# The next group's product with B moved ahead of the two products that finish a gate and up block, on VectorE

## The chip, the cores and the metric

One Trainium2 chip, one of its cores. The time is that of one launch on the device, in microseconds (us); lower is better. The engines are TensorE (PE; PEld is its weight load), VectorE (DVE), ScalarE (ACT), GpSimd (POOL) and SyncE (SP, which issues the DMAs here).

## What is computed

A block with two halves on 2048 tokens of 1024 channels, all in 32 bits. The first half is a selective scan (a state space layer), the second a gated feed-forward with low-rank (LoRA) additions:

```
h  = layernorm(x) * (1 + ca) + sa
xp = h @ x_proj_w.T                       # dt_in (32), B (16), C (16)
dt = softplus(dt_in @ dt_proj_w.T + dt_proj_b)
dA = exp(dt[..., None] * A);  dBx = dt[..., None] * B * h[..., None]
state = dA_t * state + dBx_t;  y_t = sum_n state[:, n] * C_t[n]      # over all tokens
x  = x + ga * (y + D * h)
h2 = layernorm(x) * (1 + cb) + sb
hidden = silu(gate(h2)) * up(h2)          # 1024 -> 2752, each with a LoRA term
x  = x + gb * down(hidden)                # 2752 -> 1024, with a LoRA term
```

The six modulation vectors come from `silu(c) @ wmod`, and `ga` and `gb` are kept away from zero.

## The kernel before

Channels lie on the 128 partitions (8 tiles), tokens in the free dimension. The tokens are cut into six chunks, `CH = [256, 320, 368, 368, 368, 368]`. While TensorE does the feed-forward of chunk c, the other engines do the scans of chunk c+1 and prepare chunk c+2.

**Units.** The feed-forward of a chunk is 71 units (`UNITS`): one `lora_a`, then in three parts the gate and up blocks of 128 hidden channels in turn (21 pairs and a last unit `both` with half a block each), `lora_down`, and eight `down` blocks. A unit is 24 or 25 matmuls for a gate or up block, since each 32-bit product is made of three with halved operands (high and low parts). TensorE writes a unit into one of four PSUM banks (`FP`); a fixed plan (`BANK`, `BEFORE`) says which, and which earlier use must be over (`bank_free`). The plan is made by program order.

**Groups.** The scans of a chunk are 64 groups: one of 16 states, one pair of channel tiles. For group n, VectorE makes the product with B (`dbx`, L1165: `ring <- hb * B`, B broadcast in PSUM by TensorE, L758), ScalarE makes two decays (L931), VectorE runs two scans (L1277), ScalarE keeps the last state (L948), GpSimd multiplies with C (L1414) and adds to y (L1373). The products lie in a ring of four places (`ring`); a place is free once GpSimd has added the group four before. VectorE makes the product of group n+1 just ahead of the scans of group n, both in the piece `("grp", c, n)`.

**Pieces.** Groups and the small steps of the coming chunk are spread over the units by weight (`PIECES[c][u]`). Every engine goes through the units in the same order and does, at unit u, its part of the pieces of u. The other steps that matter here: centering (`cen`, L1220) and its squares on ScalarE (L989), which TensorE sums (L735); the norm's factor (`rstd`, seed on ScalarE L996) and the product with it (`norm`, L1237); `dt` (L822), its exponent steps `sp` on ScalarE (to L1055), six products `soft` on VectorE (L1248 to L1257) and the copy `keep` (L1060); the C row copied by ScalarE (L941); low halves of weights and hidden blocks by GpSimd (L1421, L1430).

**A finished gate and up block.** For a pair of units gate j, up j: ScalarE makes the tanh of gate j (L1105) during unit up j, behind that unit's pieces. VectorE uses both in the unit after up j, by two calls of `used`: the gate's product (L1297: `(tanh + 1) * gate`), which waits for the tanh, and the up's (L1300: `0.5 * that * up`), which waits for TensorE's last matmul of the block (L877). With these two, here called the hidden products, the two banks are free. Then ScalarE rounds the result (L1117) and GpSimd makes its low half (L1430). For `both` the same is L1109, L1304 and L1307.

Of the kernel before, what the change touches and what calls it, by code (L numbers as in the profile page):

```python
# [77 lines left out]
NU = len(UNITS)  # L78
# [43 lines left out]
def group_id(c, n):  # L122
    return GROUPS * c + n
# [214 lines left out]
PIECES = [pieces_at(c) for c in range(CHUNKS)]  # L338
# [36 lines left out]
def build(nc, x_t, mod_w, cT, ident, x_proj, dt_proj, dt_bias, a_log, d_vec, w_la, w_gu, w_td, w_dn, out_t):  # L375
    w_dram = nc.dram_tensor("w_scratch", (NU, P, 2, SLOT), F32, kind="Internal").ap()

    with ExitStack() as ctx:
# [773 lines left out]
        def _(dve):  # L1152
# [38 lines left out]
                    away_from_zero(mod[:, GB, :]).then_inc(v_mod, 1)  # L1191
                dve.wait_ge(v_mod, n + 1)

            def piece(p):
                kind = p[0]
                if kind == "mod":
                    mod_vectors(p[1])
# [10 lines left out]
                elif kind == "late":  # L1208
                    blocks = LATES[p[1]]
                    n, at = blocks[0] // MOD_EACH, blocks[0] % MOD_EACH * MOD_COLS // P  # L1210
                    w = len(blocks) * MOD_COLS // P
                    dve.wait_ge(pe_col, blocks[-1] + 1)
                    V.tensor_copy(mod[:, n, at:at + w], FP[:, BANK["col", blocks[0]], 0:w]).then_inc(v_late, 1)
                elif kind == "cen":
                    _, k, c, q = p
                    if q == 0:
                        dve.wait_ge(pe_sum, ln_index(k, c) + 1)
                        if k == 0 and c >= 2:
                            dve.wait_ge(g_h2, PAIRS * (c - 1))
                    V.scalar_tensor_tensor(out=pair_of(hb, c, q), in0=over_pair(bank_of("sum", k, c)), scalar=-1.0 / D,  # L1220
                                           in1=ypair(c, q), op0=ALU.mult, op1=ALU.add).then_inc(v_cen, 1)
                elif kind == "rstd":
                    _, k, c = p
                    li = ln_index(k, c)
                    bank, row = bank_of("sq", k, c), seed[:, 0:CH[c]]
                    dve.wait_ge(a_rs, li + 1)
                    V.tensor_scalar(bank, bank, 1.0 / D, EPS, ALU.mult, ALU.add).then_inc(v_step, 1)
                    dve.wait_ge(v_step, 4 * li + 1)
                    V.scalar_tensor_tensor(out=bank, in0=bank, scalar=-0.5, in1=row, op0=ALU.mult, op1=ALU.mult).then_inc(v_step, 1)
                    dve.wait_ge(v_step, 4 * li + 2)  # L1230
                    V.tensor_tensor(bank, bank, row, ALU.mult).then_inc(v_step, 1)
                    dve.wait_ge(v_step, 4 * li + 3)
                    V.scalar_tensor_tensor(out=bank, in0=bank, scalar=1.5, in1=row, op0=ALU.add, op1=ALU.mult).then_inc(v_step, 1)
                    dve.wait_ge(v_step, 4 * li + 4)
                elif kind == "norm":
                    _, k, c, q = p
                    V.tensor_tensor(pair_of(hb, c, q), pair_of(hb, c, q), over_pair(bank_of("sq", k, c)), ALU.mult).then_inc(v_norm, 1)  # L1237
                elif kind == "xs":
                    c = p[1]
                    T = CH[c]  # L1240
                    dve.wait_ge(a_xs, c + 1)
                    V.tensor_tensor(xs[64:128, c % 2, 0:T], FP[64:128, BANK["proj", c], 0:T], xs[64:128, c % 2, 0:T].bitcast(F32), ALU.subtract).then_inc(v_xs, 1)
                elif kind == "soft":
                    _, c, i = p
                    T, t = CH[c], ND * c + i
                    bank = bank_of("dt", c, i)
                    dve.wait_ge(a_fac, NF * t + 1)
                    V.scalar_tensor_tensor(out=bank, in0=bank, scalar=FACTORS[0][1], in1=eb[:, t % 2, 0:T], op0=ALU.add, op1=ALU.mult).then_inc(v_soft, 1)  # L1248
                    for f in range(1, NF):
                        dve.wait_ge(a_fac, NF * t + f + 1)  # L1250
                        dve.wait_ge(v_soft, NF * t + f)
                        V.scalar_tensor_tensor(out=bank, in0=sqb[:, f - 1, 0:T], scalar=FACTORS[f][1], in1=bank, op0=ALU.add, op1=ALU.mult).then_inc(v_soft, 1)  # L1252
                    dve.wait_ge(v_soft, NF * (t + 1))
                    V.tensor_tensor(bank, bank, tile_of(dtb, c, i), ALU.add).then_inc(v_add, 1)
                    dve.wait_ge(v_add, t + 1)
                    dve.wait_ge(a_ini, PAIRS * c + i // 2 + 1)
                    V.scalar_tensor_tensor(out=tile_of(hb, c, i), in0=bank, scalar=modc(GA, i), in1=tile_of(hb, c, i),  # L1257
                                           op0=ALU.mult, op1=ALU.mult).then_inc(v_u, 1)
                elif kind == "first":
                    dbx(0, 0)  # L1260
                elif kind == "grp":
                    _, c, n = p
                    T = CH[c]
                    s, q = state_of(c, n)
                    g = group_id(c, n)
                    if group_after(c, n):
                        dbx(*group_after(c, n))
                    dve.wait_ge(v_dbx, g + 1)
                    if c and q == 0:
                        dve.wait_ge(a_save, 3 * NS + s + 1 if c == 1 else group_id(c - 1, n) + PAIRS)  # L1270
                    for a in range(2):
                        i = 2 * q + a
                        buf = ring_of(c, n)[:, a, :]
                        dve.wait_ge(a_da[a], g + 1)
                        if c == 0 and a == 0:
                            dve.wait_ge(a_da[1], g + 1)
                        V.tensor_tensor_scan(buf, decays(c, n, a), buf, hst[:, s * ND + i:s * ND + i + 1] if c else 0.0,  # L1277
                                             ALU.mult, ALU.add).then_inc(v_scan[a], 1)
                elif kind == "evac":
                    q, T = p[1], CH[0]  # L1280
                    dve.wait_ge(pe_y, NS * (q + 1))
                    dve.wait_ge(g_ini, PAIRS)
                    V.tensor_tensor(ypair(0, q), FP[:, 0, 0:2 * T].rearrange("p (a t) -> p a t", a=2), ypair(0, q), ALU.add).then_inc(v_ev, 1)
# [64 lines left out]
            for c in range(CHUNKS):  # L1348
                for u in range(NU):
                    g = c * NU + u  # L1350
                    last = UNITS[(g - 1) % NU][0]
                    if last == "up":
                        used(*divmod(g - 2, NU))
                    if g and last != "gate":
                        used(*divmod(g - 1, NU))
                    if UNITS[u][:2] == ("down", len(PARTS) - 1) and UNITS[u][2] == 0:
                        lora_low(c)
                    for p in PIECES[c][u]:
                        piece(p)
            used(CHUNKS - 1, NU - 1)  # L1360

        @block.gpsimd
# [146 lines left out]
```

## Time and profile before

| | |
|---|---|
| median of 3 runs | 2260.53 us (2260.38 to 2260.57) |
| the profiled execution's own time | 2265.11 us |
| its span | 2263.3 us |
| TensorE busy | 2026.9 us, 90% |
| GpSimd busy | 1558.3 us, 69% |
| VectorE busy | 1441.1 us, 64% |
| ScalarE busy | 1044.8 us, 46% |

The profiled execution is 4.6 us longer than the median. The units begin at 344 us; before that the modulation and the first chunk's scans are done. The chunks' units begin at about 344, 669, 998, 1337, 1676 and 1977 us. The last chunk's units run without any groups.

How a row is read: a time in microseconds from the span's start, a duration, engine, line, operation, output <- inputs, shapes; in brackets how long the engine had been idle before the instruction and what ended that.

### The profile page before, as it was taken

Reading aid. Unit: us, or ns where it says so; the run is one execution under the profiler, and the core shown is the slowest. Engines: PE = TensorE matmul, PEld = TensorE weight load, DVE = VectorE, ACT = ScalarE, POOL = GpSimd, SP = SyncE. Lnnn points to the kernel's source line nnn. Section 1 sums busy time; section 2 is a strip of 40 time slices with the busy share of each in tenths; the row PEclk is TensorE's granted clock in tenths of the full one; section 3 lists DMA queues with packets and bytes.
Section 4 is the critical chain, followed back from the end, with each engine's and each line's share of the span. In section 5 each row is a group of like instructions: output and inputs, shape, how many; then the busy total and the mean of one; then the engine's idle time right before and its main releaser. Section 6 shows DMA issues by size and latency. Waiting matters only on the chain.

```text
span 2263.3 us, 32653 instructions
## 1 busy us (share of the span) xinstructions
PE 2026.9 (90%) x11470; PEld 1836.5 (81%) x11470; DVE 1441.1 (64%) x2118; ACT 1044.8 (46%) x2337; POOL 1558.3 (69%) x968
## 2 busy tenths in 40 slices
PE   6597748888778889899999999999999999999999
PEld 3243227777768889899899889899889999999999
DVE  5676776778666778766778766778767774211111
ACT  3777765666453555444554443554444332210000
POOL 4679879999977877977877876877869886110100
PEclk8798768989999999999999999999999999999999
DMA  9799966778767677576667576667577877787786
GB/s 351 273 363 392 340 242 247 264 283 298 273 244 260 212 269 266 207 284 222 217 233 267 186 282 228 217 234 267 186 266 252 284 247 270 244 297 266 258 292 215
DMA packets 120051, 594.13 MB, mean 263 GB/s; under 512 B 10448, under 2 KB 22992, under 8 KB 80208
## 3 DMA queue, kind: packets, MB, share of 16 engines
q1 hardware_dynamic: 119888, 592.04, 73.4%
q8 instruction: 92, 1.51, 0.3%
q14 instruction: 71, 0.58, 0.1%
HBM read 506.97 MB, written 85.03 MB: 262 GB/s over the span
## 4 chain that ended last, share of the span: by engine, by line
PE 58%; DVE 17%; ACT 8%; POOL 7%; issue 7%; DMA 2%; DVEq 0%; ACTq 0%; SPq 0%; POOLq 0%
PE FP L852 48%; DVE ring L1277 7%; DVE ring L1165 3%; PE FP L735 3%; POOL ring L1414 3%; DVE FP L1252 2%; ACT SC L931 2%; POOL y L1373 2%; PE FP L877 1%; PE FP L813 1%; PE FP L769 1%; POOL xlo L1405 1%; DMA wts<-w_scratch 1%; DMA modw<-mod_w 1%; DVE hb L1237 1%
## 5 line engine op out<-in xcount | busy, mean ns | idle before, releaser
L852 PE MATMUL FP<-xhi,wts 128*128 128x368 f32 (+2 forms) x4224 | 1055.1, 326 | 72.2 <-ACT dtb L1060 20.9
L852 PEld LDWEIGHTS FP<-xhi,wts 128*128 128x128 f32 x4224 | 757.3, 194 | 81.1 <-issue 69.9
L1414 POOL TENSOR_TENSOR ring<-ring,c_row 128x736 f32<-128x736 f32 (+2 forms) x336 | 575.0, 1712 | 252.5 <-ACT hst L948 252.4
L852 PE MATMUL FP<-xlo,wts 128*128 128x368 f32 (+2 forms) x2112 | 685.0, 324 | 0.0
L931 ACT ACTIVATE SC<-dtb,aneg 128x368 f32<-128x368 f32 (+2 forms) x768 | 409.7, 539 | 574.5 <-DVE ring L1277 573.9
L852 PE MATMUL FP<-hhi,wts 128*128 128x368 f32 (+5 forms) x2376 | 572.6, 322 | 14.2 <-POOL hlo L1430 4.4
L1277 DVE TENSOR_TENSOR_SCAN ring<-SC,hst,ring 128x368 f32<-128x368 f32 (+1 forms) x640 | 579.9, 948 | 4.2 <-ACT SC L931 3.8
L1373 POOL TENSOR_TENSOR y<-y,ring 128x736 f32<-128x736 f32 (+1 forms) x320 | 555.6, 1736 | 13.9
L852 PEld LDWEIGHTS FP<-hhi,wts 128*128 128x128 f32 (+1 forms) x2376 | 408.5, 186 | 22.6 <-issue 10.0
L852 PEld LDWEIGHTS FP<-xlo,wts 128*128 128x128 f32 x2112 | 409.6, 194 | 1.1
L852 PE MATMUL FP<-hlo,wts 128*128 128x368 f32 (+5 forms) x1188 | 379.5, 319 | 0.0
L1165 DVE TENSOR_TENSOR ring<-hb,SC 128x736 f32<-128x736 f32 (+2 forms) x384 | 327.7, 853 | 62.9 <-PE FP L769 38.3
L1430 POOL TENSOR_TENSOR hlo<-hid,hhi 128x368 fp32r<-128x368 f32 (+4 forms) x132 | 122.4, 927 | 278.5 <-ACT hhi L1117 266.1
L852 PEld LDWEIGHTS FP<-hlo,wts 128*128 128x128 f32 (+1 forms) x1188 | 220.8, 186 | 2.3 <-issue 0.2
L1297 DVE SCALAR_TENSOR_TENSOR hid<-hid,FP 128x368 f32<-128x368 f32 (+2 forms) x126 | 64.2, 509 | 234.6 <-ACT hid L1105 230.4
L1323 DVE SCALAR_TENSOR_TENSOR y<-FP,mod,y 128x368 f32<-128x368 f32 (+2 forms) x144 | 80.9, 566 | 177.7 <-PE FP L852 177.3
L1300 DVE SCALAR_TENSOR_TENSOR hid<-hid,FP 128x368 f32<-128x368 f32 (+2 forms) x126 | 64.3, 510 | 152.7 <-PE FP L877 145.6
L948 ACT ACTIVATE hst<-ring 128x2 f32<-128x2 f32 x384 | 78.1, 203 | 141.0 <-DVE ring L1277 140.3
L758 PE MATMUL SC<-xs,sel 128*128 128x256 f32 (+2 forms) x144 | 66.1, 459 | 62.5 <-ACT c_row L941 25.6
L1105 ACT ACTIVATE hid<-FP 128x368 f32<-128x368 f32 (+2 forms) x126 | 55.4, 440 | 134.7 <-PE FP L877 134.5
L1117 ACT ACTIVATE hhi<-hid 128x368 fp32r<-128x368 f32 (+2 forms) x126 | 60.3, 479 | 119.1 <-DVE hid L1300 118.7
L758 PEld LDWEIGHTS SC<-xs,sel 128*128 128x128 f32 x144 | 30.2, 210 | 92.4 <-DVE ring L1165 31.5
(119 smaller groups left out, 2008.0 us busy)
## 6 DMA issues: line engine op xcount, KB each, us to landing
wts<-w_scratch SPq DMA_DIRECT2D x243, 1152.0 KB, 5.2
wts<-w_scratch SPq DMA_DIRECT2D x91, 896.0 KB, 4.9
wts<-w_scratch SPq DMA_DIRECT2D x51, 1024.0 KB, 5.8
w_scratch<-wts SPq DMA_DIRECT2D x43, 1152.0 KB, 8.2
modw<-mod_w SPq DMA_DIRECT2D x24, 1024.0 KB, 10.5
raw<-w_gu SPq DMA_DIRECT2D x29, 576.0 KB, 8.4
w_scratch<-wts SPq DMA_DIRECT2D x16, 896.0 KB, 8.6
w_scratch<-wts SPq DMA_DIRECT2D x9, 1024.0 KB, 6.0
```

What stands on the lines that cost most here:

```text
L735: last = mm(bank, ones[:, :], of[:, i, 0:T], start=(i == 0), stop=(i == ND - 1))
L758: mm(SC[:, BC0 + k % 2, 0:CH[c]], sel[:, at:at + 1].to_broadcast([P, P]), xs[:, c % 2, 0:CH[c]], start=True, stop=True).then_inc(pe_b, 1)
L852: last = mm(out, w, x, start=(start and k == 0 and e == 0), stop=(stop and k == n - 1 and e == 2))
L931: A(decays(c, n, a), tile_of(dtb, c, i), ACT.Exp, scale=aneg[:, i * NS + s:i * NS + s + 1]).then_inc(a_da[a], 1)
L948: A(hst[:, s * ND + 2 * q:s * ND + 2 * q + 2], ring_of(c, n)[:, :, T - 1], ACT.Copy).then_inc(a_save, 1)
L1165: V.tensor_tensor(ring_of(c, n), pair_of(hb, c, q), over_pair(SC[:, BC0 + k % 2, 0:T]), ALU.mult).then_inc(v_dbx, 1)
L1277: V.tensor_tensor_scan(buf, decays(c, n, a), buf, hst[:, s * ND + i:s * ND + i + 1] if c else 0.0, ALU.mult, ALU.add).then_inc(v_scan[a], 1)
L1300: V.scalar_tensor_tensor(out=h, in0=h, scalar=0.5, in1=bank, op0=ALU.mult, op1=ALU.mult).then_inc(v_used, 1)
L1323: V.scalar_tensor_tensor(out=y[:, c % 3, j, 0:T], in0=bank, scalar=modc(GB, j), in1=y[:, c % 3, j, 0:T], op0=ALU.mult, op1=ALU.add).then_i ...
L1373: G.tensor_tensor(ypair(c, q), ypair(c, q), ring_of(c, n), ALU.add).then_inc(g_add, 1)
L1414: G.tensor_tensor(buf, buf, over_pair(c_of(k)), ALU.mult).then_inc(g_hc, 1)
L1430: G.tensor_tensor(hlo[rows, k, 0:T], hid[rows, j % 2, 0:T], hhi[rows, k, 0:T].bitcast(F32), ALU.subtract).then_inc(g_hlo, 1)
```

## The change

At a unit that follows an up block, VectorE called `used` for the gate and for the up block first and then did the unit's pieces. Now, where such a unit has a group among its pieces, VectorE does the pieces that stand before the first group, then the product with B of the group after it, then the two calls of `used`, then the scans of the group. Units without a group, and units after another kind, keep their order. The instructions are the same ones, on the same operands and with the same waits; no other engine's program is touched.

```
-            def piece(p):
+            def piece(p, between=()):
...
                     if group_after(c, n):
                         dbx(*group_after(c, n))
+                    for unit in between:
+                        used(*unit)
                     dve.wait_ge(v_dbx, g + 1)
...
                     last = UNITS[(g - 1) % NU][0]
-                    if last == "up":
-                        used(*divmod(g - 2, NU))
+                    pieces = list(PIECES[c][u])
+                    ends = [divmod(g - 2, NU)] if last == "up" else []
                     if g and last != "gate":
-                        used(*divmod(g - 1, NU))
+                        ends.append(divmod(g - 1, NU))
+                    first = next((k for k, p in enumerate(pieces) if p[0] == "grp"), None)
+                    if first is None or last != "up":
+                        for unit in ends:
+                            used(*unit)
+                        ends, first = [], None
                     if UNITS[u][:2] == ("down", len(PARTS) - 1) and UNITS[u][2] == 0:
                         lora_low(c)
-                    for p in PIECES[c][u]:
-                        piece(p)
+                    for k, p in enumerate(pieces):
+                        piece(p, ends if k == first else ())
```

## Rows read from the trace of the kernel before

**Rows 1.** Windows: busy PE, PEld, DVE, ACT, POOL (instructions); clock, DMA share, GB/s

```profile
344.00:663.00 319.00, 260.29 (x1814) 243.50 (x1815) 232.99 (x346) 183.55 (x413) 292.88 (x188) 0.92 0.76 266
663.00:992.00 329.00, 295.97 (x1818) 281.32 (x1817) 246.23 (x339) 162.71 (x365) 257.85 (x160) 0.96 0.70 251
...
1669.00:1932.00 263.00, 259.21 (x1521) 255.94 (x1521) 175.53 (x226) 95.18 (x224) 212.31 (x130) 0.99 0.75 260
```

**Rows 2.** Waits of VectorE, 344 to 1690 us: total, times, longest

```profile
DVE hid L1297 <- ACT hid L1105: 109.3, 68, 5.1
...
DVE ring L1165 <- POOL y L1373: 11.3, 12, 2.9
```

**Rows 3.** Waits of TensorE, 663 to 1690 us: total, times, longest

```profile
PE FP L852 <- ACT dtb L1060: 10.1, 4, 3.9
PE FP L735 <- ACT dtb L989: 9.2, 3, 3.3
...
PE FP L852 <- DVE hb L1237: 7.1, 3, 3.1
PE SC L758 <- ACT c_row L941: 6.1, 5, 3.2
PE FP L822 <- ACT dtb L1060: 4.6, 3, 3.2
```

**Rows 4.** Groups by form, 344 to 1690 us: busy us, mean ns | idle

```profile
L1165 DVE TENSOR_TENSOR ring<-hb,SC 128x736 f32<-128x736 f32 x208 | 188.9, 908 | 11.8 <-PE SC L758 8.4 <-POOL y L1373 2.9
```

**Rows 5.** VectorE in order of time, unit 11 of chunk 2

```profile
1057.48 0.54 DVE L1300 SCALAR_TENSOR_TENSOR hid<-hid,FP 128x368 f32<-128x368 f32 x1 [5.18 <-PE FP L877]
1057.93 0.91 DVE L1165 TENSOR_TENSOR ring<-hb,SC 128x736 f32<-128x736 f32 x1
1058.76 1.85 DVE L1277 TENSOR_TENSOR_SCAN ring<-SC,hst,ring 128x368 f32<-128x368 f32 x2
```

**Rows 6.** TensorE in order of time: five matmuls that end a wait

```profile
490.25 0.55 PE L852 MATMUL FP<-xhi,wts 128*128 128x256 f32 x1 [3.96 <-ACT dtb L1060]
...
638.45 0.34 PE L852 MATMUL FP<-hhi,wts 128*80 128x256 f32 x1 [1.80 <-POOL hlo L1430]
...
834.32 0.39 PE L852 MATMUL FP<-xhi,wts 128*128 128x320 f32 x1 [1.28 <-ACT dtb L1060]
...
1080.91 0.41 PE L852 MATMUL FP<-xhi,wts 128*128 128x368 f32 x1 [2.01 <-DVE hb L1237]
...
1356.28 0.44 PE L852 MATMUL FP<-xhi,wts 128*128 128x368 f32 x1 [2.38 <-DMA wts<-w_scratch]
```

**Rows 7.** In order of time, unit 61 of chunk 2 and the `both` block's end

```profile
1281.50 0.54 DVE L1300 SCALAR_TENSOR_TENSOR hid<-hid,FP 128x368 f32<-128x368 f32 x1 [3.02 <-PE FP L877]
1281.95 0.92 DVE L1220 SCALAR_TENSOR_TENSOR hb<-FP,y 128x736 f32<-128x736 f32 x1
...
1285.47 0.33 PE L877 MATMUL FP<-ts,wts 128*128 128x368 f32 x1
...
1287.12 0.53 DVE L1304 SCALAR_TENSOR_TENSOR hid<-hid,FP 64x368 f32<-64x368 f32 x1 [1.65 <-ACT hid L1109]
```

**Rows 8.** Windows, columns as in the first group

```profile
1082.20:1085.60 3.40, 3.40 (x13) 3.40 (x12) 3.40 (x5) 2.71 (x6) 1.99 (x2) 0.51 0.24 97
1085.60:1089.00 3.40, 3.40 (x22) 3.14 (x21) 1.38 (x4) 3.40 (x9) 2.60 (x2) 0.99 0.17 23
834.00:837.40 3.40, 3.08 (x21) 3.11 (x22) 2.09 (x3) 2.45 (x7) 3.32 (x3) 1.00 0.83 325
360.00:480.00 120.00, 100.36 (x681) 92.34 (x680) 86.36 (x125) 70.65 (x158) 118.68 (x78) 0.93 0.77 272
```

**Rows 9.** In order of time, unit 30 of chunk 0

```profile
478.65 1.58 ACT L1055 ACTIVATE sqb<-eb,consts 128x368 f32<-128x368 f32 x3
...
481.60 0.42 DVE L1297 SCALAR_TENSOR_TENSOR hid<-hid,FP 128x256 f32<-128x256 f32 x1 [5.13 <-ACT hid L1105]
...
486.09 0.81 DVE L1165 TENSOR_TENSOR ring<-hb,SC 128x640 f32<-128x640 f32 x1
```

**Rows 10.** TensorE in order of time: its one wait for a hidden product after 663 us

```profile
742.50 0.39 PE L852 MATMUL FP<-xhi,wts 128*128 128x320 f32 x1 [0.99 <-DVE hid L1300]
```

## The prediction

> **What bounds the kernel now.** I read the windows by chunk first, then the waits of VectorE and TensorE, then the order of time at single units.
>
> The windows [rows 1] show TensorE busy 260.3 of 319 us in chunk 0 (344 to 663 us), 296.0 of 329 in chunk 1, and 259.2 of 263 in chunk 4 up to 1932 us, behind which it has no groups. There its clock is granted at 0.99. So chunk 4 is bound by TensorE alone, and chunk 5 has no scans at all. Whatever the change gives must come out of TensorE's waits in chunks 0 to 3 (chunks 2 and 3 have the same schedule and read alike). Chunk 0 has GpSimd busy 292.9 of 319 us in the same rows: there two engines share the bound.
>
> The waits of VectorE [rows 2] show what the change is about. In chunks 0 to 3 there are 84 places where a finished gate and up block is used (21 a chunk); in 68 of them VectorE stands still for ScalarE's tanh, 109.3 us in all (1.6 in the mean). Then it often waits for TensorE's last matmul of the up block too. The tanh is late because ScalarE does it behind the decays of the next group, and these wait for the scans. The product with B, the next vector work, needs neither tanh nor block, yet stands behind both.
>
> TensorE's waits [rows 3] show who would profit: from 663 us on it waits 9.2 us for squares (L989), 7.1 for the last norm (L1237), 10.1 and 4.6 for the kept dt (L1060), 6.1 for a copied C row (L941). These end chains that go through VectorE's scans. 12.8 us for the second norm's low halves (not among the rows I use) hang on work behind TensorE's own down blocks.
>
> **The change, part by part.** Nothing is added or removed. By the plan (PIECES, which the functions compute) there are 105 places after an up block, and 88 have a group in them: 17, 18, 18, 18 and 17 in chunks 0 to 4; the other 17 keep their order. At the 88 the product with B goes ahead of the two hidden products, and so does every vector piece that stands before the first group: a softplus block once (unit 30 of chunk 0), centering products at a few units.
>
> *Size of one move.* The product with B takes 0.91 us on 736 columns [rows 4], 0.81 on 640 [rows 9]. Neighbours overlap a little: at 1057.93 it starts, at 1058.76 the scans [rows 5], so it delays them by 0.83. Where VectorE stands still longer than that before the hidden products, as it does for most of the tanh waits, the scans start 0.83 us sooner and the products as before. Of the 84 places less 68, one waits for TensorE instead and one has no group; at the other 14 VectorE has no idle time, and there the scans start as before and the products 0.83 later.
>
> *Where it reaches TensorE, chunks 1 to 3.* I follow each wait back through VectorE to the last time that VectorE itself waited for TensorE, and count the moves in between.
> - Last norm (L1237), 3 waits. Behind each stand the scans of unit 11, where VectorE waits for the block (5.18 us in [rows 5]); then the seed of the norm, which ScalarE makes behind those scans' decays. One move: 3 x 0.83 = 2.5 us.
> - Kept dt before a block (L852), 4 waits. Three have only softplus places (no group, unchanged) behind them: 0. The one of 1.28 us at 834.32 [rows 6] has unit 30's move: 0.9.
> - Kept dt before the next dt (L822), 3 waits: in chunk 1 the moves of units 34 and 38, 2 x 0.83, cut to 1.6 because VectorE then meets TensorE; in chunks 2 and 3 one move is more than the wait of 0.72 and 0.71. Together 3.0.
> - C row, the one long wait of 3.2: unit 53's move, 0.9.
> - Squares (L989), 3 waits. Unit 61: one centering (0.84) and the product (0.83) both fit into the tanh wait and the 3.02 us of waiting for the block that follow [rows 7], so the scans come 1.67 sooner. But the next vector work waits for the `both` block, which ends at 1285.80, then tanh and copy: from 1287.12 it can come forward to about 1286.35. So 0.8 in chunks 2 and 3, 1.1 in chunk 1: 2.7.
>
> Sum: 2.5 + 0.9 + 3.0 + 0.9 + 2.7 = 10.0 us.
>
> *Chunk 0.* From 360 to 480 us GpSimd is busy 118.7 of 120 us [rows 8]: no gain there. At unit 30 VectorE waits 5.13 us for tanh, until 481.60, while the softplus factors are ready one by one until 480.2 [rows 9]. With softplus (3.6 us) and product ahead, VectorE reaches the hidden products at 482.7 instead of 481.60 and the scans at 483.7 instead of 486.8 (0.7 behind the product at 486.09): 3.1 us sooner. TensorE then needs the block's bank 1.1 later but no longer waits 3.96 us for the kept dt [rows 6]: 2.8 net. With the moves of units 28, 32 and 38, less what is lost where VectorE meets TensorE at unit 34, I take 4.4 us by 546 us. From 575 us GpSimd is the bound again; unit 61 (two centerings and a product) brings the squares 2.3 us sooner, but the next wait is GpSimd's low half of the hidden block, 1.80 us at 638.45 [rows 6], which stands behind its groups: GpSimd has only 0.6 idle there, so 0.6. Chunk 0: 5.0. Low end 0 (GpSimd takes it all), high end 7.7 (4.4 + 2.3 + 1).
>
> *The clock.* After the wait of 2.01 us that ends at 1080.91 [rows 6] TensorE's granted clock falls from 1.00 to 0.51 (from 2.4 to 1.2 GHz) for 3.4 us: 13 matmuls instead of 22, nine of 0.155 us, 1.4 us lost [rows 8]. The wait of 1.99 in chunk 3 is alike. After the 1.28 us that end at 834.32 the clock stays 1.00 [rows 8]. With 1.2 us left of each of the two I count both falls as gone: 2.8. Low end 0.
>
> *Costs.* A later hidden product holds a bank longer. At 742.50 TensorE already waits 0.99 us for one [rows 10]; there the seed behind unit 11's move comes 0.83 sooner and pays for it. The like wait in chunk 0 (0.91 us, unit 15) may grow by 0.8, within GpSimd's bound. Elsewhere a bank is needed one or two blocks (3 to 4 us each) later. The product can also wait for a ring place that GpSimd frees (11.3 us in 12 places, 2.9 at most [rows 2]). I take 0; the upper end is a rival.
>
> **Sum:** 10.0 + 5.0 + 2.8 = 17.8 us. The profiled execution took 2265.11 us around a span of 2263.3, so it would take 2247.3; the median of the runs is 4.6 us lower: 2260.5 - 17.8 = 2242.7.
>
> **Rivals.**
> 1. *GpSimd or TensorE takes the time back* (same). For: GpSimd's load in chunk 0, and chunk ends where TensorE waits for low halves. It needs chunk 0 to give 0, the clock nothing, and more than half of the 10 to be cut by the next wait: 2256.5 to 2260. Against: in chunks 1 to 3 GpSimd is idle some 70 us a chunk [rows 1]. 0.13.
> 2. *Products stuck behind the ring* (slower). In chunk 0 the new first instruction waits for GpSimd's addition, and with it the hidden products that free TensorE's banks; the shown waits average 0.94 us, and 12 places of chunk 0 lie in the stretches that GpSimd bounds. 12 x (0.94 + 0.81) = 21 us lost, against 10.0 + 2.8 won, if all reaches TensorE: 2268.5. It decides once the ring wait plus 0.81 passes the tanh wait by more than the banks' slack, a block of some 3 us. Against: the largest ring wait is 2.9, so hardly a place can. 0.06.
> 3. *The clock follows every shortened wait* (faster still). Falls behind the other shortened waits, about seven of 3.4 us, vanish too: 7 x 1.4 = 10 more, 2233. For: every fall from 690 us on begins behind a wait. Against: the wait of 2.38 us for a DMA at 1356.28 [rows 6] had no fall, so it is no sure thing either way. 0.13. The Trainium skill, page "TensorE: Matmul & The Clock Gate", section "HAM oscillation — how this bites in real kernels", says that an idle wait can throw the array back to half rate so that the next stretch starts slow; by it this rival is the natural outcome. The rows agree for the wait that ends at 1080.91 and not for that at 1356.28.
> 4. The main case, some 8 to 24 us: 0.68.
>
> **How the numbers follow.** 0.2% of this kernel is 4.5 us, about what a measurement can tell from nothing. Faster: main, the third rival and a little of the first, 0.81; same 0.13; slower 0.06. For the range I leave out the second rival, half of the first and half of the third: 2231 to 2257.
>
> **What the profile after would show.** The product with B directly before the gate's product, and L1300 followed by a scan at once; L1297's wait for tanh 0.8 us shorter at each place (109.3 down to about 50); TensorE's wait for the norm 2.0 to 1.2, for the squares 3.27 to 2.4, that at 490.25 gone; chunk 4 the same to 0.1 us; chunk 0 about 5 us shorter, chunk 1 5, chunks 2 and 3 3 to 4 each. The prediction is wrong if chunks 1 to 3 keep their length although the scans moved, or if new waits for L1297 or L1300 appear on TensorE.

## The result

The changed kernel took 2247.75 us in the median (2246.11 to 2249.94) against 2260.55 for the kernel before beside it: the ratio of the runs is 0.9939, with a 95% interval from 0.9923 to 0.9954, or 13.8 us less (12.8 by the medians). Predicted were 17.8. The profiled execution of the changed kernel took 2246.11 us, its span is 2244.3, so the two profiles differ by 19.0 us, of which 2.4 lie before the first unit (from run to run that stretch ends between 339 and 345 us whatever the kernel, so it is no effect of the change). Of all the runs behind this document one, of the kernel e2 below, took 4554.8 us, twice as long as the others, and is left out.

The new code has other line numbers: scan L1279, hidden products L1299 and L1302, those of `both` L1306 and L1309, additions by GpSimd L1380, products by GpSimd L1421.

First the windows by chunk, each from the matmul that begins a chunk's units to the next such one. The columns are the window, its length, then busy us (and instructions) of PE, PEld, DVE, ACT, POOL, then granted clock, DMA share and GB/s. The kernel before, chunks 0 to 3:

```profile
344.26:669.12 324.86, 261.65 (x1823) 244.61 (x1824) 237.81 (x353) 186.87 (x419) 298.74 (x191) 0.92 0.76 268
669.12:997.75 328.63, 297.11 (x1822) 282.44 (x1822) 244.72 (x338) 163.65 (x366) 256.87 (x159) 0.96 0.70 251
997.75:1336.66 338.91, 327.26 (x1821) 312.38 (x1822) 250.26 (x339) 165.59 (x366) 259.72 (x159) 0.97 0.68 236
1336.66:1675.83 339.17, 324.35 (x1821) 308.86 (x1821) 251.26 (x340) 166.35 (x367) 259.60 (x159) 0.98 0.68 236
```

The changed kernel, likewise:

```profile
341.85:664.43 322.58, 263.70 (x1824) 247.24 (x1824) 237.14 (x353) 186.37 (x419) 298.72 (x191) 0.91 0.77 272
664.43:984.57 320.14, 292.95 (x1822) 278.96 (x1822) 245.24 (x338) 163.48 (x366) 256.89 (x159) 0.97 0.72 256
984.57:1320.57 336.00, 323.09 (x1821) 307.81 (x1822) 251.35 (x339) 165.68 (x366) 259.55 (x159) 0.99 0.68 237
1320.57:1657.03 336.46, 323.85 (x1821) 309.09 (x1821) 252.02 (x340) 166.37 (x367) 259.46 (x159) 0.98 0.68 238
```

The chunks are 2.3, 8.5, 2.9 and 2.7 us shorter, and the rest (587.5 us before) 0.2. The second number to watch is TensorE's busy time. Its work is the same, so a lower busy time is a faster clock, and length less busy time is what it waited. Chunk 0 waits 4.3 us less (63.2 to 58.9) and is busy 2.1 us more. Chunks 1 to 3 together wait only 5.3 us less (58.0 to 52.7), but are busy 8.8 us less (948.7 to 939.9).

The waits of VectorE in the changed kernel, 344 to 1680 us, against [rows 2]:

```profile
DVE hid L1299 <- ACT hid L1105: 49.8, 40, 4.8
...
DVE ring L1165 <- POOL y L1380: 28.6, 30, 3.8
```

The tanh is waited for 49.8 us instead of 109.3. The ring is waited for 28.6 instead of 11.3.

The waits of TensorE, 663 to 1690 us, against [rows 3]:

```profile
PE FP L852 <- ACT dtb L1060: 9.6, 5, 3.9
PE FP L735 <- ACT dtb L989: 8.7, 3, 3.3
PE SC L758 <- ACT c_row L941: 7.4, 6, 1.7
PE FP L852 <- DVE hb L1237: 4.6, 3, 2.3
PE FP L852 <- DMA wts<-w_scratch: 4.4, 3, 3.1
PE FP L852 <- POOL hlo L1437: 3.3, 2, 2.8
...
PE FP L735 <- POOL y L1380: 1.7, 1, 1.7
PE FP L822 <- ACT dtb L1060: 1.5, 1, 1.5
```

The norm (7.1 to 4.6) and the kept dt before the next dt (4.6 to 1.5) gave in sum what was predicted. The squares hardly moved (9.2 to 8.7), the C row grew (6.1 to 7.4), and waits for GpSimd's low half (1.5 before) and for `y` (none before) took some of it back.

### The profile page after: what moved, and what is told of

Read it like the earlier page. It is cut to its first block, busy times and chain, and to the rows that moved or that the text cites. A ratio compares the mean times of both kernels' runs of the same rounds, so it can differ in the third digit from the quotient of the medians.

```text
span 2244.3 us, 32653 instructions
## 1 busy us (share of the span) xinstructions
PE 2017.0 (90%) x11470; PEld 1830.1 (82%) x11470; DVE 1442.8 (64%) x2118; ACT 1044.2 (47%) x2337; POOL 1558.1 (69%) x968
## 3 DMA queue, kind: packets, MB, share of 16 engines
q8 instruction: 92, 1.51, 0.3%
## 4 chain that ended last, share of the span: by engine, by line
PE 56%; DVE 16%; ACT 8%; POOL 8%; issue 8%; DMA 4%; SPq 0%; DVEq 0%; ACTq 0%; POOLq 0%
PE FP L852 47%; DVE ring L1279 7%; POOL ring L1421 4%; PE FP L735 3%; DVE ring L1165 3%; POOL y L1380 2%; DMA wts<-w_scratch 2%; DVE FP L1252 2%; ACT SC L931 2%; PE FP L813 1%; PE FP L877 1%; DMA out_t<-y 1%; PE FP L769 1%; DMA modw<-mod_w 1%; ACT sqb L1055 1%
## 5 line engine op out<-in xcount | busy, mean ns | idle before, releaser
L1421 POOL TENSOR_TENSOR ring<-ring,c_row 128x736 f32<-128x736 f32 (+2 forms) x336 | 575.8, 1714 | 233.4 <-ACT hst L948 233.1
L1279 DVE TENSOR_TENSOR_SCAN ring<-SC,hst,ring 128x368 f32<-128x368 f32 (+1 forms) x640 | 580.1, 949 | 4.2 <-ACT SC L931 3.8
L1380 POOL TENSOR_TENSOR y<-y,ring 128x736 f32<-128x736 f32 (+1 forms) x320 | 554.8, 1734 | 13.9
L1437 POOL TENSOR_TENSOR hlo<-hid,hhi 128x368 fp32r<-128x368 f32 (+4 forms) x132 | 122.2, 926 | 279.8 <-ACT hhi L1117 267.4
L1302 DVE SCALAR_TENSOR_TENSOR hid<-hid,FP 128x368 f32<-128x368 f32 (+2 forms) x126 | 64.3, 510 | 157.8 <-PE FP L877 151.3
L1299 DVE SCALAR_TENSOR_TENSOR hid<-hid,FP 128x368 f32<-128x368 f32 (+2 forms) x126 | 64.1, 508 | 158.0 <-ACT hid L1105 157.3
L1105 ACT ACTIVATE hid<-FP 128x368 f32<-128x368 f32 (+2 forms) x126 | 55.5, 441 | 137.0 <-PE FP L877 136.6
L1117 ACT ACTIVATE hhi<-hid 128x368 fp32r<-128x368 f32 (+2 forms) x126 | 60.3, 479 | 118.5 <-DVE hid L1302 118.0
```

Of the source, the lines that this page charges most:

```text
L1302: V.scalar_tensor_tensor(out=h, in0=h, scalar=0.5, in1=bank, op0=ALU.mult, op1=ALU.mult).then_inc(v_used, 1)
L1380: G.tensor_tensor(ypair(c, q), ypair(c, q), ring_of(c, n), ALU.add).then_inc(g_add, 1)
L1421: G.tensor_tensor(buf, buf, over_pair(c_of(k)), ALU.mult).then_inc(g_hc, 1)
L1437: G.tensor_tensor(hlo[rows, k, 0:T], hid[rows, j % 2, 0:T], hhi[rows, k, 0:T].bitcast(F32), ALU.subtract).then_inc(g_hlo, 1)
```

## The experiments

Twelve kernels ran, each 4 to 12 times beside the kernel before. Their profiles, one of each kernel, are read like the two above (us; "waits" is length less TensorE's busy time):

| | median | ratio, 95% interval | chunk 0: length, waits | chunks 1 to 3: length, waits, busy |
|---|---|---|---|---|
| before (profile 2265.1) | 2260.5 | | 324.9, 63.2 | 1006.7, 58.0, 948.7 |
| the change | 2247.8 | 0.9939 [0.9923, 0.9954] | 322.6, 58.9 | 992.6, 52.7, 939.9 |
| e1 | 2246.8 | 0.9938 [0.9927, 0.9950] | 322.5, 59.4 | 995.2, 55.0, 940.2 |
| e2 | 2257.9 | 0.9985 [0.9976, 0.9994] | 325.5, 60.9 | 1001.7, 61.8, 939.9 |
| e3 | 2252.5 | 0.9957 [0.9943, 0.9972] | 324.2, 58.7 | 1000.4, 60.6, 939.7 |
| e4 | 2223.4 | 0.9830 [0.9817, 0.9842] | 316.2, 56.2 | 977.4, 40.0, 937.4 |
| e5 | 2252.8 | 0.9962 [0.9949, 0.9976] | 325.1, 62.6 | 997.1, 58.2, 938.9 |
| e6 | 2258.8 | 0.9984 [0.9973, 0.9995] | 326.1, 60.3 | 998.7, 51.8, 946.9 |
| e7 | 2229.3 | 0.9858 [0.9845, 0.9870] | 316.4, 54.9 | 982.3, 43.8, 938.5 |
| e8 | 2231.4 | 0.9868 [0.9852, 0.9884] | 316.2, 58.4 | 984.3, 46.2, 938.0 |
| e9 | 2225.1 | 0.9845 [0.9823, 0.9866] | 318.0, 53.6 | 975.9, 39.8, 936.2 |
| e10 | 2226.2 | 0.9844 [0.9823, 0.9864] | 319.2, 54.6 | 974.9, 39.0, 935.9 |
| e11 | 2233.2 | 0.9877 [0.9859, 0.9896] | 318.9, 57.6 | 987.4, 46.1, 941.3 |
| e12 | 2225.4 | 0.9841 [0.9827, 0.9855] | 317.4, 58.2 | 978.9, 41.3, 937.6 |

The kernel before beside them took 2261.2 (e1 to e4), 2260.95 (e5 to e8), 2261.3 (e9 to e11) and 2260.9 us (e12).

### e1 and e2: the seventeen traced places, and the other 71

The prediction traced TensorE's waits back to the moves at 17 of the 88 places: units 28, 30, 32, 38 and 61 of chunk 0; 11, 30, 34, 38, 53 and 61 of chunk 1; 11, 38 and 61 of chunks 2 and 3. Kernel e1 has the new order at these alone, e2 at all others alone.

```
-                    if first is None or last != "up":
+                    if first is None or last != "up" or not ((c, u) in TRACED):      # e1
+                    if first is None or last != "up" or (c, u) in TRACED:            # e2
```

> The new order only at the 17 places whose moves I traced to a wait of TensorE before the result (chunk 0: units 28, 30, 32, 38, 61; chunk 1: 11, 30, 34, 38, 53, 61; chunks 2 and 3: 11, 38, 61); the other 71 keep the old one. Theory A (the gain is made at those places): the whole gain stays, 2246 to 2250 us. Theory B (any shift of the order changes where GpSimd, DMA and clock meet, and the gain is spread or drawn by luck): about 17/88 of 13.8 us, so 2258.

> The complement: the new order at the 71 places that I did not trace to a wait of TensorE. Theory A: nothing, 2258 to 2262 us. Theory B: about 71/88 of the gain, 2249. If it is slower than 2262, late hidden products cost (rival 2).

Measured: 14.4 us gained by e1, 3.3 by e2. The 17 places bring all that the change brings (13.8), within the intervals, as theory A says. The other 71 are worth 0.15% (0.06 to 0.24), at the edge of what theory A allowed and far from theory B. So the step of following TensorE's waits back to the moves picked the places that count.

It didn't get every wait right, though. In e2, which has none of the traced moves, the norm's waits from 663 us on are 4.9 us instead of 7.1, and those before the next dt 2.6 instead of 4.6. TensorE waits more there for hidden products (3.7 us instead of 1.0), for GpSimd's low halves (4.0 instead of 1.5) and for the C row (8.2 instead of 6.1). So the sooner scans of the other places do reach TensorE, but other waits take back what they give. And the two short waits before the dt of chunks 2 and 3 (0.72 and 0.71 us), which the prediction gave to the move of unit 38, are still there in e1, which has that move:

```profile
1178.55 0.43 PE L822 MATMUL FP<-xs,dhi 128*128 128x368 f32 x1 [0.72 <-ACT dtb L1060]
...
1515.61 0.44 PE L822 MATMUL FP<-xs,dhi 128*128 128x368 f32 x1 [0.70 <-ACT dtb L1060]
```

In e2 and in the change they are gone. So moves that weren't traced took them away.

### e3: the product alone

At a place where the pieces before the first group hold softplus or centering products, the change moves these too. Here only the product with B goes ahead of the hidden products.

```
+                    made = bool(first)
+                    if made:
+                        if group_after(*pieces[first][1:]):
+                            dbx(*group_after(*pieces[first][1:]))
+                        for unit in ends:
+                            used(*unit)
+                        ends = []
```

> Only the product with B goes ahead; softplus and centering pieces that stand before the first group stay behind the hidden products. Theory A: at unit 30 of chunk 0 the 3.1 us become 0.8, and the squares of unit 61 of chunk 0 come 0.8 instead of 2.3 sooner, but GpSimd takes that one back; chunks 1 to 3 lose 0 to 0.3 us each at unit 61. So 1 to 3 us slower than the change, 2249 to 2251. Theory B: no different from the change, 2246 to 2250.

Measured: 8.7 us gained by the medians (2261.2 less 2252.5), or 9.7 by the ratio. Either way that is 4.1 us less than the change gained, which would be the worth of the softplus of unit 30 and the few centerings that went along. It is more than the 1 to 3 us of theory A. But the interval of e3 begins at 0.9943 and that of the change ends at 0.9954, so they overlap, and even theory B isn't excluded.

### e4 and e7: the softplus and norm pieces too

At the 17 places after an up block without a group the change keeps the old order. At 12 of them VectorE has softplus or norm products, which need no tanh either. Kernel e4 is the change with these ahead of the hidden products as well, e7 with the softplus alone.

```
-                    if first is None or last != "up":
+                    late = first is None and last == "up" and any(p[0] in ("soft", "norm") for p in pieces)
+                    if (first is None or last != "up") and not late:
...
                         piece(p, ends if k == first else ())
+                    if late:
+                        for unit in ends:
+                            used(*unit)
```

> The change, and in addition the softplus and norm pieces go ahead of the hidden products where a unit after an up block has no group (8 softplus and 4 norm places). Theory A: the waits that the change left alone (3.88, 2.47 and 2.47 us for the kept dt, 2.28, 1.17 and 1.16 for the norm, 3.70 in chunk 0) lose most of their length: 8 to 16 us faster than the change, 2232 to 2240. Theory B, or later hidden products holding banks: no gain over the change, 2246 or more, with new waits of TensorE for L1299 or L1302.

> The change, and softplus (not norm) ahead of the hidden products at the 8 units after an up block that have no group. By the run with both (25 us faster than the change), less the norm's waits of 2.28, 1.17 and 1.16 us of which the C row's waits behind them took 2.5 back in chunk 1: softplus holds nearly all, 2224 to 2230. If the norm pieces carry half, 2235.

Measured: e4 took 2223.4 us, 24 us less than the change and more than the 8 to 16 of theory A, and e7 2229.3, as expected. The softplus brings 18.5 of these 24. In e4 TensorE's waits from 663 to 1690 us have these rows left:

```profile
PE SC L758 <- ACT c_row L941: 10.0, 6, 3.4
PE FP L735 <- ACT dtb L989: 8.7, 3, 3.3
...
PE FP L822 <- ACT dtb L1060: 0.5, 1, 0.5
PE FP L852 <- ACT dtb L1060: 0.2, 1, 0.2
```

The wait for the kept dt before a block is 0.2 us instead of 9.6, and the norm's wait is not in the list any more. The C row's wait takes back a part (7.4 to 10.0). What was worth most was not among the moves: the softplus, a chain of six products that TensorE waits for at its end, stood behind the tanh at places without a group.

### e5 and e6: the change from chunk 1 on, and at unit 61 alone

```
-                    if first is None or last != "up":
+                    if first is None or last != "up" or not (c > 0):      # e5
+                    if first is None or last != "up" or u != 61:          # e6
```

> The change in chunks 1 to 4 only. By my terms chunks 1 to 3 hold 10.0 of 15.0 us without the clock, so 2250 to 2252. If the two ends of chunk 0's chain (softplus of unit 30, unit 61 and the weight loads behind it) carry as much as the profile after suggests (4.0 us to the first wait of chunk 1, and 2.2 more by a clock fall that is gone there), then this run lacks 6 of the 13.8 us: 2252 to 2255, and its wait for weights near 686 us is back at 5 to 7 us.

> The new order at unit 61 of chunks 0 to 3 only (centering and product ahead of the hidden products). My step: 0.6 us in chunk 0 and 2.7 in chunks 1 to 3, 3.3 together: 2257. Rival from the profile after: the wait for squares shrinks in chunks 0 and 1 but GpSimd's low half of the hidden block takes it, and in chunks 2 and 3 nothing moves: 2259 to 2261, within noise.

Measured: e5 gained 8.1 us, so chunk 0 has 5.1 us of the change by the medians, where 5.0 were predicted; the two intervals overlap a little, so this is rough, and 2252.8 doesn't tell the two expected ranges apart. The wait for weights at the start of chunk 1 is back, at 6.4 us. In chunks 1 to 3 e5's profile is 9.6 us shorter than that of the kernel before, yet TensorE waits there as long (58.2 and 58.0 us): all of it is less busy time. e6 gained 2.2 us (3.6 by the ratio), between its two expectations, where the prediction has 0.6 + 2.7 for unit 61. By its profile e6 waits 9.0 us less than the kernel before (112.2 against 121.2 in chunks 0 to 3) while TensorE is busy 2.3 us more: one profile each doesn't price an edit as small as this.

### e8: ScalarE's tanh first, VectorE in the old order

The tanh was late because ScalarE does it behind the pieces of its unit, decays among them. This is the kernel before with that one call moved in ScalarE's program, and VectorE's program as it was.

```
-                    for p in PIECES[c][u]:
-                        piece(p)
                     if last == "gate":
                         before(*divmod(g - 1, NU))
+                    for p in PIECES[c][u]:
+                        piece(p)
```

> The kernel before with ScalarE's tanh ahead of its unit's pieces instead of behind them; VectorE keeps the old order. If the tanh is late only because it stands behind the decays (my reading of the 68 waits), VectorE no longer waits for it and the scans come 1.1 to 1.6 us sooner at each place in a chain: as good as the change or better, 2238 to 2248. Rival: ScalarE then waits for TensorE's gate block with the decays queued behind, scans come later where VectorE runs ahead, and it is slower than before, 2262 to 2275.

Measured: 2231.4 us, 29.5 less than before and 16 less than the change, and so better than the 2238 to 2248 expected; the rival is out. ScalarE and VectorE in order of time at a pair of units of chunk 2 in e8:

```profile
1026.23 0.46 ACT L1105 ACTIVATE hid<-FP 128x368 f32<-128x368 f32 x1
1026.88 0.57 ACT L931 ACTIVATE SC<-dtb,aneg 128x368 f32<-128x368 f32 x1 [0.19 <-DVE ring L1277]
...
1027.64 0.51 DVE L1297 SCALAR_TENSOR_TENSOR hid<-hid,FP 128x368 f32<-128x368 f32 x1
...
1034.69 0.54 DVE L1300 SCALAR_TENSOR_TENSOR hid<-hid,FP 128x368 f32<-128x368 f32 x1 [6.54 <-PE FP L877]
...
1035.15 0.91 DVE L1165 TENSOR_TENSOR ring<-hb,SC 128x736 f32<-128x736 f32 x1
...
1036.99 0.57 ACT L931 ACTIVATE SC<-dtb,aneg 128x368 f32<-128x368 f32 x1 [8.51 <-DVE ring L1277]
```

The tanh (L1105) starts at 1026.23, ahead of the decays at 1026.88, so VectorE's L1297 at 1027.64 waits for nothing; then VectorE stands still for TensorE's block (6.54 us before L1300 at 1034.69), and the product with B still comes behind it. One of the waits of VectorE in the kernel before, 344 to 1690 us, and two in e8, 344 to 1680 us:

```profile
DVE hid L1300 <- PE FP L877: 48.8, 18, 5.6
```

```profile
DVE hid L1300 <- PE FP L877: 97.8, 45, 7.8
...
DVE hid L1297 <- ACT hid L1105: 13.2, 13, 1.7
```

The 109.3 us for the tanh are 13.2 us, but VectorE waits 97.8 us for the block instead of 48.8. So the order on VectorE could still matter here, which the next kernels ask.

### e9, e10 and e11: do the cures add up?

e9 is the change with the tanh first. e10 is e4 with the tanh first. e11 is e10 with VectorE's product with B in its old place at the units with a group:

```
-                    if (first is None or last != "up") and not late:
+                    if not late:
```

> The change, with ScalarE's tanh put ahead of its pieces of the kept dt and the decays as in e8. Theory A: moving VectorE's product and moving ScalarE's tanh are two cures for one stall (VectorE's hidden product waits for a tanh, and TensorE for the hidden product), so with the tanh early the 13.8 us of the product's move shrinks to 0 to 5 us more than e8's 29.5: 2226 to 2232 us, ratio 0.985 to 0.987. Theory B: the two stalls are separate and their gains add up: 2260.95 less 29.5 less 13.8 gives 2217.6, ratio 0.981. Between them 2222 decides.

> The change, VectorE's softplus and norm pieces ahead as in e4, and ScalarE's tanh ahead as in e8. Theory A: the kept dt's waits are cured by e4 and by e8 alike, and only the norm's waits (1.7 + 0.8 + 0.8 us left in e8) and a part of chunk 0's are new here: 2217 to 2224 us, ratio 0.981 to 0.984, which is no more than e4 alone. Theory B: e4's 24.6 us over the change and e8's 29.5 us over the kernel before add up with the change's own 13.8: 2261 less 67.9, some 2193 us, ratio 0.970. Between them 2208 decides.

> As e10, but without the move that is studied: the product with B stays behind the two products of the finished block, only the softplus and norm pieces and the tanh are ahead. Theory A: with the tanh early, VectorE's hidden product is no longer held, so that the product with B gets to its turn in time in either place: within 4 us of e10 (2217 to 2228 us). Theory B: the move keeps its own worth of about 13.8 us: e10 plus 10 to 15 us.

Measured: 2225.1, 2226.2 and 2233.2 us. The kernels with both the softplus move and the tanh move are no faster than those with one: e10 against e4 and e9, e11 against e8. These two cure the same waits, as theory A says (e10 is no faster than e4, if 2 us over its range) and theory B doesn't. With the product it is otherwise. It is worth 6.4 us from e8 to e9 and 7.0 from e11 to e10, more than the 0 to 4 or 5 of theory A and half of the 13.8 of theory B. For e9 theory B is out: its 2217.6 us lies below the interval, which begins at 2221. Otherwise the times alone don't decide, since the intervals within each pair overlap. The windows for chunk 0 and for chunks 1 to 3 together, of e8 and then of e9, show where the halves are:

```profile
339.81:655.97 316.16, 257.76 (x1823) 242.10 (x1824) 237.11 (x352) 186.65 (x418) 298.71 (x191) 0.92 0.78 275
655.97:1640.22 984.25, 938.04 (x5462) 893.21 (x5463) 743.01 (x1016) 492.92 (x1096) 776.20 (x475) 0.98 0.70 246
```

```profile
338.62:656.59 317.97, 264.38 (x1824) 247.65 (x1824) 235.37 (x351) 185.95 (x418) 298.66 (x191) 0.91 0.78 276
656.59:1632.50 975.91, 936.15 (x5462) 892.61 (x5463) 747.34 (x1017) 493.51 (x1097) 775.79 (x475) 0.99 0.71 248
```

Chunks 1 to 3 are 8.3 us shorter in e9, chunk 0 is 1.8 us longer. From e11 to e10 it is the same picture, 12.4 shorter and 0.4 longer. In chunk 0 of e8 GpSimd is busy 298.7 of 316.2 us.

### e12: the tanh first, the product ahead from chunk 1 on

This was run to try that reading: e9, with chunk 0 in the old order on VectorE.

```
-                    if first is None or last != "up":
+                    if first is None or last != "up" or c == 0:
```

> ScalarE's tanh first as in e8, and the new order of the product with B only from chunk 1 on, so chunk 0 keeps the old order. Reading C, from the windows by chunk: in chunks 1 to 3 the move keeps its worth with the tanh early (8.4 us from e8 to e9, 12.4 from e11 to e10), because VectorE then waits for the block, and the product fills that wait; in chunk 0 GpSimd, busy 298.7 of 316 us, sets the length, and the move gives nothing or costs up to 2 us. So chunk 0 is as long as in e8 (316.2) or up to 1 us off, chunks 1 to 3 together some 976 us as in e9 (975.9) against 984.2 in e8, and the time 2222 to 2226 us, a ratio of 0.983 to 0.985. Reading A, in which the two moves cure one stall: chunks 1 to 3 at 982 us or more, and 2229 us or more.

Measured: 2225.4 us, with chunk 0 at 317.4 and chunks 1 to 3 at 978.9 us. Reading C holds (by time and ratio; the chunks are 0.2 and 3 us over what it gave) and A is out, since the interval ends at 2228: with the tanh early, the product ahead gives nothing in chunk 0 that these profiles show (e8 and e12, with the same order there, differ by 1.2 us), and in chunks 1 to 3 it is worth some 5 to 12 us by the profiles and 6 to 7 by the medians. The fastest kernels here, e4, e9, e10 and e12 (2223 to 2226 us), can't be told apart. Of them e9 has the shortest diff, and e4 doesn't touch ScalarE's program.

## Why the prediction was right, and which terms were not

**What bounds the kernel, and what can't change.** Right: the last two chunks are the same (587.5 and 587.3 us), and everything came from TensorE's waits and its clock in chunks 0 to 3.

**The size of one move, 0.83 us.** Right. VectorE in order of time at unit 11 of chunk 2 in the changed kernel, against [rows 5]:

```profile
1037.51 0.92 DVE L1165 TENSOR_TENSOR ring<-hb,SC 128x736 f32<-128x736 f32 x1 [1.97 <-PE SC L758]
1038.35 0.53 DVE L1299 SCALAR_TENSOR_TENSOR hid<-hid,FP 128x368 f32<-128x368 f32 x1
1044.18 0.54 DVE L1302 SCALAR_TENSOR_TENSOR hid<-hid,FP 128x368 f32<-128x368 f32 x1 [5.30 <-PE FP L877]
1044.63 1.85 DVE L1279 TENSOR_TENSOR_SCAN ring<-SC,hst,ring 128x368 f32<-128x368 f32 x2
```

The product with B is made at 1037.51, ahead of the wait for the block (5.30 us), and the scans start 0.45 us behind the start of L1302, where it had been 1.28. The norm's three waits fell by 2.5 us as predicted, the wait of 1.28 at 834.32 to 0.49, those before the next dt from 4.6 to 1.5 (predicted 3.0 less, though 1.4 of it not by the move that the prediction names, as e1 shows). A later hidden product costs what the prediction says, too: in e2, where unit 11 of chunk 1 keeps the old order, the wait of 0.99 us at 742.50 is 1.82, 0.83 longer, and in the changed kernel it is 1.00.

**The squares, 2.7 predicted, 0.5 measured.** This term failed, and by a cause that the prediction lacks. It took the vector work behind the `both` block to come 0.8 us sooner. The start did: in the changed kernel VectorE's L1306 starts 0.94 us behind the start of the block's last matmul (at 1269.34), before it was 1.65. But the next product took the gain back. VectorE and GpSimd in order of time, the kernel before:

```profile
1287.62 0.95 POOL L1430 TENSOR_TENSOR hlo<-hid,hhi 128x368 fp32r<-128x368 f32 x1
1287.68 1.28 DVE L1307 SCALAR_TENSOR_TENSOR hid<-hid,tda 64x368 f32<-64x368 f32 x1
1288.54 2.04 POOL L1373 TENSOR_TENSOR y<-y,ring 128x736 f32<-128x736 f32 x1
```

The changed kernel, likewise:

```profile
1269.85 0.97 POOL L1437 TENSOR_TENSOR hlo<-hid,hhi 128x368 fp32r<-128x368 f32 x1
...
1270.28 0.53 DVE L1306 SCALAR_TENSOR_TENSOR hid<-hid,FP 64x368 f32<-64x368 f32 x1 [2.60 <-ACT hid L1109]
1270.78 1.75 POOL L1380 TENSOR_TENSOR y<-y,ring 128x736 f32<-128x736 f32 x1
1270.85 2.07 DVE L1309 SCALAR_TENSOR_TENSOR hid<-hid,tda 64x368 f32<-64x368 f32 x1
```

The product L1309 takes 2.07 us where its twin L1307 took 1.28. Both read `hid` and `tda`, two tiles in SBUF. Each ends some 0.4 us behind an instruction of GpSimd that ran when it began: 1288.96 behind 1288.57 before, 1272.92 behind 1272.53 in the changed kernel. L1306, with one input in PSUM, took its 0.53 us beside GpSimd's L1437. In chunk 1 of the kernel before the same product took 0.48 us, where the running GpSimd instruction ended 0.09 us behind its start. In chunks 0 to 3 of all fourteen profiles, 56 cases, it ended 0.26 to 0.40 us behind the end of the GpSimd instruction that ran when it began, while the next one was running. So it acts as if held until the running instruction is over. By coming 0.8 us sooner it met the next instruction of GpSimd, of 1.75 us, at its start.

e3 shows what the term is worth without that meeting. VectorE's product in chunk 2 and TensorE's matmul that waits for the squares there, in e3:

```profile
1280.61 1.18 DVE L1309 SCALAR_TENSOR_TENSOR hid<-hid,tda 64x368 f32<-64x368 f32 x1
...
1284.35 1.81 PE L735 MATMUL FP<-dtb,ones 128*128 128x368 f32 x5 [2.45 <-ACT dtb L989]
```

Here it began in a GpSimd instruction of 0.97 us, took 0.89 us less than in the changed kernel, and the squares' wait is 0.89 us shorter than there (2.45 for 3.34 us). That is the 0.8 less than before (3.27) that the prediction gave to this chunk, and chunk 3 is alike (2.39, 3.28 and 3.21). The next wait took it back in e3: 2.07 and 2.14 us for the low half. The Trainium skill, page "GPSIMD Engine Reference", section "1. Specifications", says that GpSimd's access to SBUF is shared with VectorE and that they contend when a VectorE instruction has two SBUF inputs; the trace agrees in these rows. No run gave this product another input, so that its second SBUF input is the reason wasn't tried. In chunk 1 of the changed kernel the squares' wait did fall (2.75 to 2.09), but the wait for the low half of the hidden block rose from 1.12 to 2.84.

**The C row, 0.9 predicted, 1.3 lost.** The one long wait fell as said and more (3.20 to 1.53). But in chunks 2 and 3 a new one came. TensorE in order of time, two matmuls of chunk 2 and one of chunk 3 in the changed kernel:

```profile
1066.78 0.41 PE L852 MATMUL FP<-xhi,wts 128*128 128x368 f32 x1 [1.18 <-DVE hb L1237]
...
1076.20 0.43 PE L758 MATMUL SC<-xs,sel 128*128 128x368 f32 x1 [1.49 <-ACT c_row L941]
...
1411.90 0.43 PE L758 MATMUL SC<-xs,sel 128*128 128x368 f32 x1 [1.69 <-ACT c_row L941]
```

The norm's wait ends at 1066.78, and at 1074.71, 7.9 us later, TensorE wants ScalarE's copy of the C row and waits 1.49 us, until 9.4 us behind the norm. Before, TensorE needed 1.4 us more for that stretch, at half clock [rows 8], and came 9.3 us behind the norm, when the row was as good as there (in chunk 3 it waited 0.18 us). So of the two falls that the prediction counted as gone, both went, and their 2.8 us were spent on this wait (1.49 and 1.69 us). In e1 and in e2 the same two waits stand there (1.49 and 1.48 in chunk 2, 1.69 in chunk 3). It had been covered by the slow clock; the prediction looked for a wait standing next behind the gain only in chunk 0.

**The direct waits of chunks 1 to 3 together, 10.0 predicted, 5.3 measured** (58.0 to 52.7), with 3.8 of these for weights (8.2 to 4.4), most of it the wait at the start of chunk 1 that chunk 0's gain shortened (5.80 to 3.07). Counted as the prediction counts, with that wait given to chunk 0, 2.6 us stand against the 10.0. By the rows of waits, norm, dt and kept dt gave 2.5 + 3.1 + 0.5 = 6.1 and the squares 0.5; the C row (1.3), the low half (1.8), `y` (1.7) and L1299 (0.6) took 5.4 back.

**Chunk 0, 5.0 predicted, 4.0 measured** to the end of the wait for weights at the start of chunk 1 (347.3 us from the chunk's start before, 343.3 in the changed kernel); 5.1 by the medians of e5 and the change. The wait of 3.96 us at unit 30 is gone. At unit 61 the wait for the squares is 2.76 instead of 5.11 us and that for the low half 4.34 instead of 1.80, so GpSimd took the gain back, as predicted.

**The clock, 2.8 predicted, 6.8 in the profiles** (8.8 less busy time in chunks 1 to 3, 2.1 more in chunk 0). Here the third rival came in part. Windows of 3.4 us in the kernel before, each behind one of TensorE's waits:

```profile
691.60:695.00 3.40, 3.40 (x13) 3.40 (x14) 0.49 (x1) 0.89 (x3) 3.32 (x3) 0.50 1.02 431
...
917.40:920.80 3.40, 3.40 (x16) 3.40 (x17) 3.30 (x6) 0.57 (x1) 3.32 (x3) 0.65 0.35 146
...
1147.40:1150.80 3.40, 3.40 (x13) 3.40 (x13) 3.40 (x5) 1.83 (x5) 1.96 (x2) 0.54 0.09 29
```

The changed kernel, behind the same waits, and the last behind chunk 3's twin of the third:

```profile
685.20:688.60 3.40, 3.40 (x23) 3.40 (x24) 3.10 (x4) 1.85 (x5) 3.40 (x3) 1.00 1.01 425
...
902.80:906.20 3.40, 3.38 (x23) 3.39 (x24) 3.30 (x6) 1.24 (x3) 3.40 (x3) 1.00 0.75 306
...
1133.20:1136.60 3.40, 3.40 (x22) 3.40 (x21) 3.40 (x5) 2.59 (x7) 2.81 (x2) 1.00 0.10 37
...
1468.80:1472.20 3.40, 3.40 (x13) 3.40 (x12) 3.40 (x5) 2.53 (x6) 2.80 (x2) 0.51 0.09 35
```

Behind the shortened waits at 691.57 (5.80 to 3.07 us) and 917.39 (3.20 to 1.53) the falls towards half clock are gone, and likewise behind 863.58 (3.20 to 1.51; clock 0.53 and then 1.00) and the norm in chunk 2, which had 0.51 [rows 8]. But the wait for the kept dt in chunk 2, 2.51 us before and 2.47 in the changed kernel, had a fall before and has none now, and its twin of 2.47 in chunk 3 (the last row) has one. So a shortened wait can save the clock, but the clock also differs behind a wait that is unchanged, and which falls go was not to be foreseen from the lengths. How much of the 6.8 us is the change stays open. TensorE's busy time in chunks 1 to 3 is 948.7 in the profile of before, 946.9 in e6 and 936 to 941 in all the others, even in e2 with its small gain, and the profiled execution of before was 4.6 us longer than the median. A part of it is in every run: the mean granted clock is 0.947 over the 54 runs of the kernel before that stood beside the experiments, 0.947 over e2's, and 0.950 over the four runs of the changed kernel. The measured 13.8 us would fit waits of 9.6 us (4.3 + 5.3) and some 4 of clock, but e5, whose gain of 8.1 us comes with no shorter waits in its profile, says that the share of the clock may be larger. How the gain is divided between the two isn't shown.

So the total was off by 4 us, with the waits 5.4 us too high (9.6 for 15.0) and the clock too low. The direction, the seventeen places and the size of one move were right. The sum came out near because two misses partly cancel, and that is luck: in chunks 1 to 3 the waits gave a quarter of their 10.0, and the clock, counted at 2.8, gave more than that by each of these readings.

**The rivals.** The second can be dropped: the ring is waited for 17 us more, but TensorE's waits for a hidden product are 1.0 and 0.6 from 663 us on, where they had been 1.0, and 6.7 us in chunk 0, where they had been 8.8. (Its own sum gives 2268.7, not 2268.5.) The first was at work in the squares and low halves, and took about a third of the predicted 15 us of waits, not nearly all. The third was half right.

## What to carry to other kernels

Behind an in-order engine, ask first who makes the thing that it waits for and what that engine does ahead of it: moving ScalarE's short tanh ahead of its decays brought twice what reordering VectorE around the late tanh did, by one moved call. Follow TensorE's waits back to single places, which picks those that count (17 of 88 gave all within the noise, if not always by the wait that was named), and look there for every piece that doesn't need the late input, not just the one that the change names: the softplus was worth more than the product. Take off a part of each shortened wait for the next one that stood covered behind it (here a third), and where a VectorE instruction reads two SBUF tiles beside a busy GpSimd, as the second product of `both` does, price a wait for GpSimd's running instruction. One profile of each kernel isn't enough to divide a gain of some 10 us between waits and clock.

## What the runs showed of the hardware

- VectorE's second product of `both`, with both inputs in SBUF, took 0.48 us (64x320) to 2.08 us (64x368) according to what GpSimd was doing; in 56 of 56 cases it ended 0.26 to 0.40 us behind the end of the GpSimd instruction that ran when it began. It had been counted as fixed work.
- TensorE's granted clock fell to half behind some waits of 2.5 us and not behind others of the same length (0.54 behind 2.51 us, and behind 2.47 us 1.00 at one place and 0.51 at another), and TensorE's busy time for the same matmuls of chunks 1 to 3 ranged from 935.9 to 948.7 us over the fourteen profiles.
